# Splitting the cached keys before they are transposed, on ScalarE and GpSimd, in the stage that quantises the first weight

## The reference, cut to what matters

```
# L0: a quantised linear layer with a low-rank correction
delta = lora_B @ lora_A * 0.5
normalized = (weight + delta).reshape(512, 4, 128) / exp(scale_log)
quantized  = cb[searchsorted((cb[:-1] + cb[1:]) * 0.5, normalized)]   # 64 codebook values
w_eff = (quantized * scale).reshape(512, 512) + delta
x = x + x @ w_eff.T                                                    # x: 64 x 32 x 512

# L1: attention over a paged cache: 64 pages of 32 keys, 8 heads of 128, and 16 pages a batch
q, k, v = x @ Wq.T, x @ Wk.T, x @ Wv.T          # 32 query heads, 8 key heads
q, k = rope(rmsnorm(q)), rope(rmsnorm(k))
scores = q @ [k_cache[block_table], k].T / sqrt(128)      # masked beyond cache_seqlens
x = x + softmax(scores) @ [v_cache[block_table], v] @ Wo.T
```

## Time and profile before

| | |
|---|---|
| time, median of 3 runs | 2333.78 us (2333.56 to 2333.95) |
| the profiled execution: its time, its span | 2333.03 us, 2331.4 us |
| PE, PE weight load busy | 2190.5 us, 1425.2 us |
| DVE, ACT, POOL busy | 1745.9, 1472.9, 1245.9 us |
| first slices of 58 us each, PE busy tenths | 5 8 8 6 |
| the same slices, DVE busy tenths | 6 9 9 5 |
| mean DMA rate over the span | 180 GB/s |

### The profile page before, as it was taken

One profiled execution on the slowest core, in us unless ns is written; L12 is line 12 of the kernel. 1 busy time (PEld: TensorE's weight loads), 2 busy tenths in 40 slices (PEclk: granted clock), 3 DMA queues, 4 the chain that ended last, 5 costly groups with the idle time before them and its releaser, 6 DMA issues. The chain is left out here.

```text
span 2331.4 us, 61112 instructions
## 1 busy us (share of the span) xinstructions
PE 2190.5 (94%) x18068; PEld 1425.2 (61%) x18068; DVE 1745.9 (75%) x3942; ACT 1472.9 (63%) x4968; POOL 1245.9 (53%) x2066
## 2 busy tenths in 40 slices
PE   5886789999999999999998789999999999999997
PEld 2443456666666666666665456666666666666664
DVE  6995468777777777777777377777777777777774
ACT  2542367676666666676765466667677666666663
POOL 4330036666666666666664146666666666666562
PEclk9997889999999999999999899999999999999999
DMA  2785666566666666566654665666566666666563
GB/s 100 241 297 161 220 203 178 175 177 177 183 176 185 181 177 180 177 179 178 174 174 130 204 184 171 182 178 177 177 178 180 184 184 179 178 179 177 169 185 108
DMA packets 445186, 419.55 MB, mean 180 GB/s; under 512 B 51615, under 2 KB 371437, under 8 KB 444846
## 3 DMA queue, kind: packets, MB, share of 16 engines
q1 hardware_dynamic: 399726, 277.08, 40.5%
q0 software_dynamic: 40960, 134.25, 19.1%
q10 hardware_dynamic: 4160, 4.19, 0.5%
HBM read 369.12 MB, written 46.21 MB: 178 GB/s over the span
## 5 line engine op out<-in xcount | busy, mean ns | idle before, releaser
L767 POOL DMA_INDIRECT pages<-values_split,rows_s x512 | 516.8, 1009 | 133.3 <-issue 119.8
L1018 PE MATMUL PR<-Wt,xT 128*128 128x512 f16 x2304 | 559.6, 381 | 3.7 <-DVE Wt L1268 3.7
L1104 ACT ACTIVATE pts<-PTp 128x512 f16<-128x512 f32 x512 | 306.7, 599 | 341.4 <-PE PTp L975 277.4
L998 PEld LDWEIGHTS Op<-pts,pages 128*128 128x128 f16 x6144 | 383.3, 98 | 137.6 <-DVE OT L1227 19.3
L998 PE MATMUL Op<-pts,pages 128*128 128x128 f16 x6144 | 427.3, 219 | 17.5 <-DVE OT L1227 12.1
L964 PE MATMUL Sp<-pages,qT 128*128 128x512 f16 x1536 | 417.0, 380 | 7.1 <-PEq L178 6.6
L1110 ACT ACTIVATE masked<-masked,small 128x544 f32<-128x544 f32 x512 | 380.4, 743 | 58.8 <-DVE small L1209 43.7
L1214 DVE TENSOR_TENSOR pts<-PTp,pts 128x512 f16<-128x512 f32 x512 | 351.8, 687 | 86.9 <-ACT pts L1104 50.8
L1209 DVE CUSTOM_DVE_ANT_0 masked<-Sp,mask 128x544 f32<-128x544 f32 x512 | 369.9, 722 | 51.2 <-PE Sp L967 30.8
L1039 PE MATMUL WOp<-WoT,OT 128*128 128x512 f16 x1536 | 379.7, 382 | 9.8 <-PEq L178 9.8
L1018 PEld LDWEIGHTS PR<-Wt,xT 128*128 128x128 f16 x2304 | 225.9, 98 | 200.1 <-issue 9.9
(11 more groups left out here) (196 smaller groups left out, 3070.8 us busy)
## 6 DMA issues: line engine op xcount, KB each, us to landing
pages<-keys_transposed SPq DMA_DIRECT2D x2048, 64.0 KB
mask<-mask_rows SPq DMA_DIRECT2D x128, 128.0 KB
v<-new_values SPq DMA_DIRECT2D x96, 128.0 KB
pages<-in_L_cond_Wq SPq DMA_DIRECT2D x9, 1024.0 KB, 7.3
keys_transposed<-pages SPq DMA_DIRECT2D x32, 256.0 KB, 3.0
values_split<-pages SPq DMA_DIRECT2D x16, 512.0 KB, 3.5
xT<-x_transposed SPq DMA_DIRECT2D x32, 256.0 KB
pages<-values_split,rows_s POOLq DMA_INDIRECT x512
```

Of the source, the lines that this page charges most:

```text
L767: nc.gpsimd.indirect_dma_start(out=vS[:, n % 2, c, :, :].rearrange("p l n -> p (l n)"), out_offset=None, in_=v_d, in_offset=bass.IndirectO ...
L998: nc.tensor.matmul(o, vS[:, par, c, low, h * D:(h + 1) * D], pts[:, u % 2, part, c * P:(c + 1) * P], start=(k == 0), stop=False)
L1018: m = nc.tensor.matmul(bank(k), xb[:, c, xl, :], Wp[:, c, wl, GROUP_COL[k]:GROUP_COL[k] + HID], start=(i == 0), stop=(i == NPASS - 1))
L1104: nc.scalar.activation(pts[:, u % 2, 0, :], PTp[:, :], ACT.Copy).then_inc(G.pt_hi, 1)
```

## The change

The order of two steps is exchanged: the keys are split first, in their loaded form, and the float16 parts are transposed.

- ScalarE, at j = 2n, `split_keys(n)`: rounds 128x512 of `kin` to float16 into a new pair of buffers `ksp` (SBUF). It waits for the load and for `turn(n - 2)`.
- GpSimd, `keys_low(n)`: subtracts, from `kin` and `ksp`, both in SBUF, 128x512. Two of them stand ahead of each chunk's value subtraction in GpSimd's loop.
- TensorE, after sum j = 2n + 3 (two later than before): `turn(n)` waits for `keys_low(n)` and makes 8 float16 transposes of 128x128 in place of 4 float32 ones, into the same bank seen as float16.
- ScalarE, at j = 2n + 4, `keys_out(n)`: copies both parts out of the bank, two instructions.
- VectorE has no part in it; its 32 subtractions go.
- SyncE's load of chunk c + 3 waits for the key splits in place of the turns, and the key store waits for `kt_done`.

```diff
--- before.py
+++ after.py
@@ -154,7 +154,7 @@
...
-            ... "vin_2", "kt_turned", "kt_hi", "kt_lo", "v_hi", "v_lo",
+            ... "vin_2", "ks_hi", "ks_lo", "kt_turned", "kt_done", "v_hi", "v_lo",
...
             "n5_high", "n5_done", "c5_done", "p5_done", "v5_loaded_0", "v5_loaded_1", "pages_bounded", "pages_stored", "vn_stored", "v5_zero",
@@ -369,6 +369,8 @@
         kst_stored, vst_stored = [G.kst_0, G.kst_1], [G.vst_0, G.vst_1]
         q_bank = [Sp[:, 0:512], Sp[:, 512:1024], PR[:, 0, :], PR[:, 1, :]]
         t_bank = [Op[:, :], PTp[:, :], WOp[:, :]]
+        ksp = [pages3[:, 2048 + 1024 * r:3072 + 1024 * r].rearrange("p (l n) -> p l n", l=2) for r in range(2)]
+        t_half = [m.bitcast(F16).rearrange("p (l n) -> p l n", l=2) for m in t_bank]
         weT = pages[:, 0:4096].rearrange("p (c l n) -> p c l n", c=IC, l=2)
         NC = PAGES // PPC
         NI = NC * HALVES
@@ -377,7 +379,7 @@
             def _(sp):
                 def load(c):
                     if c >= 3:
-                        sp.wait_ge(G.kt_turned, 2 * (c - 2))
+                        sp.wait_ge(G.ks_lo, 2 * (c - 2))
                         sp.wait_ge(G.v_lo, c - 2)
                     sp.dma_start(kin[c % 3], k_chunks[c]).then_inc(kin_loaded[c % 3], 16)
                     sp.dma_start(vin[c % 3], v_chunks[c]).then_inc(vin_loaded[c % 3], 16)
@@ -394,7 +396,7 @@
                 for c in range(NC):
                     for f in range(HALVES):
                         n = HALVES * c + f
-                        sp.wait_ge(G.kt_lo, n + 1)
+                        sp.wait_ge(G.kt_done, 2 * (n + 1))
                         sp.dma_start(kT_d[f * PAGES + PPC * c:f * PAGES + PPC * (c + 1), :, :].rearrange("q d x -> d q x"),
                                      kst[n % 2].rearrange("p q h l n -> p q (h l n)")).then_inc(kst_stored[n % 2], 16)
                     sp.wait_ge(G.v_lo, c + 1)
@@ -416,12 +418,12 @@
             @block.tensor
             def _(pe):
                 def turn(n):
-                    c, f = n // HALVES, n % HALVES
-                    pe.wait_ge(kin_loaded[c % 3], 16 * (c // 3 + 1))
+                    pe.wait_ge(G.ks_lo, n + 1)
                     if n >= 3:
-                        pe.wait_ge(G.kt_lo, n - 2)
-                    for h in range(KVH):
-                        m = nc.tensor.transpose(t_bank[n % 3][:, h * P:(h + 1) * P], kin[c % 3][:, (f * KVH + h) * D:(f * KVH + h + 1) * D], ident[:, :])
+                        pe.wait_ge(G.kt_done, 2 * (n - 2))
+                    for part in range(2):
+                        for h in range(KVH):
+                            m = nc.tensor.transpose(t_half[n % 3][:, part, h * P:(h + 1) * P], ksp[n % 2][:, part, h * D:(h + 1) * D], ident16[:, :])
                     m.then_inc(G.kt_turned, 1)
                 for j in range(NJ):
                     pe.wait_ge(G.mask16_done, j + 1)
@@ -437,14 +439,15 @@
                             m = nc.tensor.matmul(q_bank[k], diag[:, j % DRING, part, :], mask16[j % RING][:, k * 512:(k + 1) * 512],
                                                  start=(j == 0 and part == 0), stop=False)
                     m.then_inc(G.summed, 1)
-                    if j % 2 == 1:
-                        turn(j // 2)
+                    if j % 2 == 1 and j >= 3:
+                        turn(j // 2 - 1)
+                turn(NI - 2)
                 turn(NI - 1)
 
                 for k in range(4):
                     pe.wait_ge(G.weff_done, k + 1)
                     if k < 3:
-                        pe.wait_ge(G.kt_lo, NI - 2 + k if k < 2 else NI)
+                        pe.wait_ge(G.kt_done, 2 * (NI - 2 + k if k < 2 else NI))
                     else:
                         pe.wait_ge(G.weff_lo, 1)
                     for ic in range(IC):
@@ -453,11 +456,19 @@
 
             @block.scalar
             def _(a):
-                def keys_high(n):
+                def split_keys(n):
+                    c, f = n // HALVES, n % HALVES
+                    a.wait_ge(kin_loaded[c % 3], 16 * (c // 3 + 1))
+                    if n >= 2:
+                        a.wait_ge(G.kt_turned, n - 1)
+                    nc.scalar.activation(ksp[n % 2][:, 0, :], kin[c % 3][:, f * KVH * D:(f + 1) * KVH * D], ACT.Copy).then_inc(G.ks_hi, 1)
+
+                def keys_out(n):
                     a.wait_ge(G.kt_turned, n + 1)
                     if n >= 2:
                         a.wait_ge(kst_stored[n % 2], 16 * (n // 2))
-                    nc.scalar.activation(kst[n % 2][:, :, :, 0, :], t_bank[n % 3].rearrange("p (h q n) -> p q h n", h=KVH, q=PPC), ACT.Copy).then_inc(G.kt_hi, 1)
+                    for part in range(2):
+                        nc.scalar.activation(kst[n % 2][:, :, :, part, :], t_half[n % 3][:, part, :].rearrange("p (h q n) -> p q h n", h=KVH, q=PPC), ACT.Copy).then_inc(G.kt_done, 1)
 
                 def values_high(c):
                     a.wait_ge(vin_loaded[c % 3], 16 * (c // 3 + 1))
@@ -487,9 +498,12 @@
                         a.dma_start(rope_d[ts_, :, w * 2 * D:(w + 1) * 2 * D].rearrange("t p n -> p t n"), rope_t[w][:, ts_, :, :].rearrange("p t e n -> p t (e n)")).then_inc(G.table_stored, 16)
                     if j % 4 == 0:
                         values_high(j // 4)
-                    if j % 2 == 0 and j >= 2:
-                        keys_high(j // 2 - 1)
-                keys_high(NI - 1)
+                    if j % 2 == 0:
+                        split_keys(j // 2)
+                    if j % 2 == 0 and j >= 4:
+                        keys_out(j // 2 - 2)
+                keys_out(NI - 2)
+                keys_out(NI - 1)
                 for k in range(4):
                     a.wait_ge(G.weff_turned, k + 1)
                     nc.scalar.activation(weT[:, :, 0, k * P:(k + 1) * P], t_bank[(NI + k) % 3].rearrange("p (c n) -> p c n", c=IC), ACT.Copy, scale=WS).then_inc(G.weff_hi, 1)
@@ -545,15 +559,10 @@
                     if step % 4 == 3:
                         m.then_inc(G.table_done, 1)
 
-                def keys_low(n):
-                    v.wait_ge(G.kt_hi, n + 1)
-                    V.tensor_tensor(kst[n % 2][:, :, :, 1, :], t_bank[n % 3].rearrange("p (h q n) -> p q h n", h=KVH, q=PPC), kst[n % 2][:, :, :, 0, :], ALU.subtract).then_inc(G.kt_lo, 1)
                 for j in range(NJ):
                     if j >= RING:
                         v.wait_ge(G.summed, j - RING + 1)
                     V.tensor_scalar(mask16[j % RING], norm, thr[:, j:j + 1], None, ALU.is_gt).then_inc(G.mask16_done, 1)
-                    if j % 2 == 1 and j >= 5:
-                        keys_low((j - 5) // 2)
                     if 10 <= j <= 24 and j % 2 == 0:
                         angles((j - 10) // 2)
                     if 30 <= j <= 44 and j % 2 == 0:
@@ -564,7 +573,6 @@
                     if j == 48:
                         v.wait_ge(G.mask_table, 17)
                         V.tensor_scalar(mask_tab, iota_k[0:B, :], seq_colf, NEG, ALU.is_ge, ALU.mult).then_inc(G.mask_table, 1)
-                keys_low(NI - 3)
 
                 def weff_low(k):
                     v.wait_ge(G.weff_hi, k + 1)
@@ -583,8 +591,6 @@
                                     scale_t[:, 4 * k:4 * k + 4].rearrange("p (g o) -> p g o", o=1).to_broadcast([P, 4, P]), ALU.mult).then_inc(G.weff_chain, 1)
                     v.wait_ge(G.weff_chain, 3 * k + 3)
                     V.tensor_tensor(a_, a_, delta[:, c0:c1], ALU.add).then_inc(G.weff_done, 1)
-                    if k < 2:
-                        keys_low(NI - 2 + k)
                     if k >= 1:
                         weff_low(k - 1)
                 weff_low(3)
@@ -616,7 +622,13 @@
                         link(Q.tensor_scalar(rows[pr, f * NB4:(f + 1) * NB4], src, float(PSIZE * HALVES), tiny[pr, 10 + f:11 + f], ALU.mult, ALU.add))
                     Q.tensor_scalar(pos[pr, :], seqf[pr, 0:B].rearrange("p (t q) -> p t q", q=4)[:, :, q], piota[pr, :], None, ALU.add).then_inc(G.positions, 1)
                     g.wait_ge(G.positions, q + 1)
+                def keys_low(n):
+                    c, f = n // HALVES, n % HALVES
+                    g.wait_ge(G.ks_hi, n + 1)
+                    nc.gpsimd.tensor_tensor(ksp[n % 2][:, 1, :], kin[c % 3][:, f * KVH * D:(f + 1) * KVH * D], ksp[n % 2][:, 0, :], ALU.subtract).then_inc(G.ks_lo, 1)
                 for c in range(NC):
+                    keys_low(2 * c)
+                    keys_low(2 * c + 1)
                     g.wait_ge(G.v_hi, c + 1)
                     nc.gpsimd.tensor_tensor(vst[c % 2][:, :, 1, :], vin[c % 3].rearrange("p (f n) -> p f n", f=HALVES), vst[c % 2][:, :, 0, :], ALU.subtract).then_inc(G.v_lo, 1)
         clear()
```

(2 more changed lines are left out.)

## The result

The changed kernel takes 2348.68 us (median of 6 runs, 2343.77 to 2355.47) against 2333.67 (6 runs, 2330.86 to 2333.95): a ratio of 1.0069, 95% interval 1.0052 to 1.0085, 15 us slower. A second measurement gave 1.0079 (1.0058 to 1.0100). The forecast was 2352.5 and slower.

A forecast was written before the change was run, and what follows sets the result against it. VectorE bounds from 54.3 to 148 us, TensorE from 148 to 178.9. Last mask 19.3 us later, tail -0.6: +18.7 on 2333.0 is 2351.7, the median 0.75 higher, so 2352.5; range 2341 to 2362, down to 2338 for rival 2.

The forecast's parts named there:

- The exclusion: VectorE's masks and GpSimd's subtractions block each other: 14 value subtractions x 1.88 = 26.3 us, 27 key subtractions x 0.9 = 24.3.
- The mask group: VectorE's group of 63 masks in the changed profile: busy time about 130 us in place of 102.8.
- VectorE's relief: VectorE loses 32 key subtractions of 0.61 us a step, its one work that could lie under GpSimd.
- ScalarE's round: ScalarE's loop through the value store: 9.2 us a chunk, pacing chunks without angles or tables, 4 us more.
- The start: Before GpSimd's loop, row numbers delay the first key split to 51.7 us; TensorE's sum 7 is done at 62.0.
- Rival 2: Key subtractions hidden; ScalarE's 9.2 us loop paces all 13.3 chunks after 62.0; last mask 184, 2339 us; chance 0.17.
- rival 1: Key subtractions cost masks nothing, no ScalarE loop; TensorE bounds from 62.0; last mask 169, 2324 us; chance 0.11.
- The last mask: End of VectorE's last mask in the stage: forecast at 197.3 us, 19.3 later than in the trace before.
- The tail: From the last mask through the weight chain to the stage's end: -0.6 us, between -2.6 and +1.
- The turns: TensorE's 8 float16 transposes in place of 4 float32: 0.44 us a turn in both, between -0.1 and +0.3 for 32.
- The clock: TensorE at the stage's start: pairs of 1.01 us at 29.76 taken as 1.2 GHz, 0.63 at 34.83 as 2.4 GHz.
- Rival 3: TensorE pauses 3 us in each chunk and falls to 1.2 GHz: 39 us above the forecast, 2391; chance 0.05.

## Why the prediction was right

- **The exclusion.** Right, and it is the main cause. From 61.75 us to the last mask at 189.4 the masks, angles and tables took 127.65 us, 80.6 of their own by the forecast's steps and 1.8 of waiting: 45.2 went to GpSimd, where the forecast had 50.6. In that time fell 12 value and 26 key subtractions, where it had counted 14 and 27. At 1.88 us a value subtraction, each key subtraction cost 0.87, forecast 0.9; the run with the values stored first gives 0.89 in the same way. So the price held and the count was too high. Leaving them out gave back 0.77 us each; VectorE then waits for the ring (4.5 us from 54 to 165), which may hide the rest (argued, not shown).
- **The mask group** was forecast at about 130 us of busy time and has 108.6: of the 45.2 us some 31 fell on the 53 masks (94.9 less 63.6), the other 14 on angles and tables.
- **VectorE's relief.** With GpSimd's key subtractions and ScalarE's round both gone the stage is 13.3 us shorter than before. In the changed kernel that gain is inside the sum and doesn't show.
- **The start.** The times came within half a microsecond (first split at 51.7, the turn began at 51.83; sum 7 at 62.0 against 61.55). What it was worth the forecast never priced by itself. In the trace of before, sum 12 starts at 65.1 us, after at 69.8: only 4.7 us of the pause of 12.3 are a loss, as the kernel before stood in the same place behind GpSimd's numbers. Mending it gave 4.6 or 3.9, by the profile that it is laid beside (4.0 by the ratios).
- **ScalarE's round.** The length of 9.2 us was right to a tenth, its place and its effect weren't: +4 in the sum, 0.6 to -0.1 in the run that takes it away. In that run the last mask ends at 193.5, and 193.2 is the forecast's sum without the round. So the round added nothing to the masks. With it they ended 4.1 us earlier, and the tail was 4.7 longer. Why the masks then lost less isn't shown; fewer of GpSimd's subtractions fell on them (38 against 40).
- The round was no small thing all the same: it kept the run without subtractions at 2340.4. Rival 2 had 2339, but by a last mask at 184 and a short tail; it was at 176.6 with 27.1 us behind it, so that the number agrees is luck. With both limits gone the kernel is at 0.9953 of before, 2323 on the scale of the first measurement; rival 1 had 2324.
- **The last mask** came at 189.4, forecast 197.3: 4 for the round, 5.4 for what GpSimd took, 0.3 for the start, less 1.8 of waiting.
- **The tail** was mis-sized the other way: 24.3 us from the last mask to the next block against 20.3 before, +4.0, forecast -0.6. TensorE was behind (VectorE waited 3.96 for the first bank), and GpSimd's last subtractions stretched three instructions of the chain by 3.1 us; the bound of +1 was too tight.
- **The turns** cost the same in float16: 0.61 us for eight against 0.60 for four.
- **The clock.** Rival 3 is out: the granted clock was 0.97 from 54.3 to 148 us and 1.00 from 148 to 178.9. The 1.2 GHz that the prediction gives the pair at 29.76 rests on its length alone; the profile has a granted clock of 1.00 there, where the restart at 51.83 has the same pace at 0.50. No run here shows why.
- The stage was forecast 18.7 us longer and was 15.4. The last mask was 7.9 too late and the tail 4.6 too short in the forecast: that the sum came so near is in part luck.
- By the Trainium skill (SBUF — State Buffer, on the shared port pair) the loser of the pair waits for the whole instruction. Single rows agree nearly (1.9 us for a value subtraction of 2.13); the mean price of 0.87 us for a key subtraction of 1.15 lies under it, as a subtraction costs nothing where VectorE waits for the ring (argued, not shown).

What stays open: the part of the span behind the stage differed between 2124 and 2137 us over these profiles, by instructions that are the same, and no run here shows why. It is as large as most differences above, so those of the stage are the firmer ones, though each is of one profile.

## What to carry to other kernels

Moving a subtraction from VectorE to GpSimd is no relief while VectorE runs masks like these, or instructions with two SBUF inputs, beside it: count most of GpSimd's time onto VectorE's (here 1.88 of 2.13 us and 0.87 of 1.15), and see whether what is taken away was the part that could run beside GpSimd. Where two limits lie close, taking one away shows only the gap to the next (10.0 and 0.6 us alone, 28.7 together): work out the length of each round through a store and a queue, and take them away together before calling one harmless. And look at what stands ahead of a loop on an engine before putting new work into it: mending only that order beat both kernels.

## What the hardware showed that I had not expected

VectorE's instructions with two SBUF inputs are stretched too; the prediction had only seen GpSimd wait for them. One of 1.21 us took 2.18 beside a key subtraction (84.80, above) and another 3.14 beside a value subtraction, in the timeline of the changed kernel:

```profile
118.78 3.11 POOL L633 TENSOR_TENSOR pages<-pages 128x1024 f16<-128x1024 f32 x1
...
119.83 3.14 DVE L556 SCALAR_TENSOR_TENSOR OT<-Wt,wq_b 128x1024 f32<-128x1024 f32 x1
```

It lost 1.9 us, as much as a mask does, which has twice its elements: in these rows what is lost goes by GpSimd's instruction. It is also why putting the key subtraction back on VectorE, out of SBUF, didn't end the exclusion: a subtraction of 0.68 us took up to 2.42.
